# A loop of two steps for GpSimd's gathers in the edge loop of a graph attention layer

## What is computed

```python
h = (layernorm(x) @ W.T).reshape(n, 8, 32)
alpha = a_src . h[src] + a_dst . h[dst] + sum(relu(edge_attr @ edge_W.T + edge_b) * h[dst])
alpha = where(alpha >= 0, alpha, 0.2 * alpha)
ex = exp(alpha - segment_max(alpha, dst)[dst])
out = segment_sum(h[src] * ex / segment_sum(ex, dst)[dst], dst)
x = x + out + bias          # then the mixture of experts on layernorm(x)
```

## Time and profile before

| | us |
|---|---|
| median of 3 runs | 3645.68 |
| lowest and highest run | 3639.31, 3689.38 |
| the profiled execution | 3650.59 |
| its span, first to last instruction | 3648.7 |

### The profile page before, as it was taken

One profiled execution on the slowest core, in us unless ns is written; L12 is line 12 of the kernel. 1 busy time (PEld: TensorE's weight loads), 2 busy tenths in 40 slices (PEclk: granted clock), 3 DMA queues, 4 the chain that ended last, 5 costly groups with the idle time before them and its releaser, 6 DMA issues. The chain is left out here.

```text
span 3648.7 us, 35893 instructions
## 1 busy us (share of the span) xinstructions
PE 2371.3 (65%) x8642; PEld 1602.4 (44%) x8642; DVE 2272.9 (62%) x3546; ACT 985.6 (27%) x2822; POOL 1902.5 (52%) x2041
## 2 busy tenths in 40 slices
PE   1646766766666665766676766756666464269998
PEld 1424443433444443443444434434344243068887
DVE  7956776766667676776667767766666564352223
ACT  3522222222222222222222222222222221053332
POOL 3655655665665555565556655665555453507000
PEclk9857777777777777778767777787777777559999
DMA  8345555555555555555555545555555985200000
GB/s 272 111 136 140 155 144 142 148 144 156 155 151 142 151 143 146 140 149 163 147 137 154 150 133 143 154 149 164 147 141 148 119 121 83 79 14 24 17 20 30
DMA packets 341605, 471.09 MB, mean 129 GB/s; under 512 B 115596, under 2 KB 262718, under 8 KB 341170
## 3 DMA queue, kind: packets, MB, share of 16 engines
q0 software_dynamic: 90000, 262.14, 29.1%
q1 hardware_dynamic: 250578, 206.73, 19.8%
q10 hardware_dynamic: 848, 0.26, 0.0%
HBM read 380.17 MB, written 88.72 MB: 129 GB/s over the span
## 5 line engine op out<-in xcount | busy, mean ns | idle before, releaser
L999 POOL DMA_INDIRECT src_in<-t_node_rows,rec_in x1760 | 1678.7, 954 | 1230.2 <-DVE weighted L1256 635.9
L1061 PE MATMUL p_sum<-weighted,hot 128*128 128x264 f32 x3520 | 1207.8, 502 | 567.9 <-issue 366.6
L1061 PEld LDWEIGHTS p_sum<-weighted,hot 128*128 128x128 f32 x3520 | 841.1, 249 | 924.6 <-issue 595.2
L1206 DVE SCALAR_TENSOR_TENSOR prod<-p_enc,near 128x512 f32<-128x512 f32 x880 | 563.1, 681 | 577.8 <-ACT near L1128 316.1
L1256 DVE TENSOR_TENSOR weighted<-src_in,p_turn 128x1024 f32<-128x1024 f32 x440 | 534.6, 1215 | 295.8 <-remote 111.7
L1039 PE MATMUL p_pick<-win,hotT 128*128 128x272 f32 x880 | 389.5, 531 | 369.5 <-ACT near L1128 170.2
L1210 DVE TENSOR_REDUCE dots<-prod 128x32 f32<-128x1024 f32 x440 | 536.9, 1220 | 15.2
L1108 ACT ACTIVATE hot<-apart 128x128 f32<-128x128 f32 x440 | 136.2, 310 | 1299.9 <-PE p_sum L1061 604.3
L1128 ACT COPY near<-p_pick 128x272 f32<-128x272 f32 x440 | 169.4, 385 | 821.8 <-remote 494.6
L1039 PEld LDWEIGHTS p_pick<-win,hotT 128*128 128x128 f32 x880 | 156.6, 223 | 478.2 <-issue 297.8
L1032 PE MATMUL p_enc<-expander,attrT 30*128 30x256 bf16 x1760 | 310.6, 302 | 39.7 <-DMA attrT<-t_block_attr 37.8
(11 more groups left out here) (334 smaller groups left out, 1627.9 us busy)
## 6 DMA issues: line engine op xcount, KB each, us to landing
win<-t_node_rows SPq DMA_DIRECT2D x440, 136.0 KB
t_block_sums<-sums SPq DMA_DIRECT2D x110, 528.0 KB
places<-t_block_places SPq DMA_DIRECT2D x110, 256.0 KB
src_in<-t_node_rows,rec_in POOLq DMA_INDIRECT x1760
attrT<-t_block_attr SPq DMA_DIRECT2D x330, 36.0 KB
t_node_rows<-out_rows SPq DMA_DIRECT2D x49, 136.0 KB, 1.8
x<-in_x SPq DMA_DIRECT2D x4, 1536.0 KB, 25.6
out_x<-x SPq DMA_DIRECT2D x48, 128.0 KB
```

What stands on the lines that cost most here:

```text
L999: pool.indirect_dma_start(src[:, q.par, b, k, :], None, scr["rows"], bass.IndirectOffsetOnAxis(ap=rec_i[:, q.par, b, k:k + 1], axis=0)).th ...
L1061: last = nc.tensor.matmul(p_sum[b % 2][:, 0:ROW], hot[:, q.par, b, :], weighted[:, b, k, :], start=(k == 0), stop=(k == W - 1))
L1206: nc.vector.scalar_tensor_tensor(prod[:, 2 * half:2 * half + 2, :], p_enc[(PAIRS * b + half) % len(p_enc)][:, :, :], 0.0, near[:, q.par, b ...
```

## The change

POOL's steps of the edge loop are no longer written out one by one. A new function `loop` writes out the steps 0 and 1, then one `Fori` on POOL with (110 - 2 - 2) / 2 = 53 turns, whose body holds two steps, and then, as before, the last two steps and the early gathers of the merge (`last`). The steps in the body have expressions in the loop's register as `s` and `turn`; `par` stays a number, so the addresses of tiles and the semaphores of the gathers stay fixed. The values of the five waits of a step become expressions in the register. All other engines still use `steps`.

```diff
@@ -867,6 +867,16 @@
                 body(straight(k))
             last()
 
+        def loop(engine, body, last):
+
+            for k in range(RING):
+                body(straight(k))
+            turns = (STEPS - RING - 2) // RING
+            with engine.Fori(0, turns) as i:
+                for u in range(RING):
+                    body(Step(i * RING + RING + u).of(i + 1, u))
+            last()
+
         assert STEPS % RING == 0 and Q == 4
 
         turn = P // Q
@@ -1013,7 +1023,7 @@
-            steps(gather, last)
+            loop(nc.gpsimd, gather, last)
 
         @block.tensor
```

## The result

| us | before | after |
|---|---|---|
| median of 4 runs each | 3662.84 | 3719.83 |
| lowest and highest | 3639.31, 3689.38 | 3699.99, 3853.15 |
| the profiled execution | 3650.59 | 3705.42 |
| its span | 3648.7 | 3703.7 |

The account below looks back on a forecast made before the run. The prediction took the semaphore round between PE, ACT and DVE to bound each step, gathers beside it. From 3650.6 us, -5 for pauses, 0 for registers, 0 for turns gave 3645.6, as a median 3641 us; range 3612 to 3695.

Parts of the forecast that it names:

- Step 1, the pauses: POOL's gathers in the edge loop: program-fetch pauses, 28 us in all, vanish; a fifth, 5 us, gained.
- rival C: POOL's pauses count in full: 28 us back, 3618 us (0.12), or 3573 with half of SP's waits (0.04).
- Step 2, registers: POOL's register operations before the edge loop's waits: at most 64 us, hidden by the sequencer's lead, costed at 0.
- Step 3, the turn: POOL's jump back at the 53 loop turns: up to 74 us if refetched, but short body, costed at 0.
- rival A: Each of POOL's 53 turns costs a pause of 1.4 or 2.8 us: 3720 or 3794 us; chance 0.09.
- rival B: Smoother POOL lengthens slow times of SP and ACT by 15%, 74 us on ACT's waits: 3715 us; chance 0.04.
- the term for the slow times: POOL's register operations while sequencers are slow: 1.4 us per group, 148 us bound without lead, costed at nothing.

Follow-up runs that it names:

- e2: The changed kernel with POOL's loop turning only twice, 52 steps written out per turn, registers kept in the waits, against the kernel before: 3691.92 us, ratio 1.0093.
- e3: The written-out kernel before, with block 0's gathers also waiting for block 1's weighting, against the kernel before: 3888.17 us, ratio 1.0616.
- e8: The written-out kernel before, with block 0's gathers also waiting for DVE's next prod pair, about 1.3 us later, against the kernel before: 3749.81 us, ratio 0.9945.

## Why the prediction was wrong, point by point

**What bounds the kernel.** "What bounds a step is this round of semaphores between PE, ACT and DVE; the gathers run beside it" holds as a reading of the chip of the profile: after the change the gathers' landing is again only 56.6 us of DVE's idle time. What the sentence left out is how the gathers act on the round. They do not delay it as a predecessor; where they run on this chip, the news in it comes late (10% of SP's records slow at the start of a run of gathers, 51% from the ninth on). The chips C and D show the difference: without the slow times the same round is short enough that the gathers bound the loop.

**Step 1, the pauses (5 us gained).** Wrong in its cause. The pauses of 1.70 us are still there with a body of two steps that runs 53 times. POOL's timeline of the kernel after:

```profile
1375.97 0.94 POOL L1009 DMA_INDIRECT src_in<-t_node_rows,rec_in  x1 [0.43 <-issue]
1378.61 0.94 POOL L1009 DMA_INDIRECT src_in<-t_node_rows,rec_in  x1 [1.70 <-issue]
...
2397.22 0.94 POOL L1009 DMA_INDIRECT src_in<-t_node_rows,rec_in  x1 [0.82 <-DVE weighted L1266]
2399.86 0.95 POOL L1009 DMA_INDIRECT src_in<-t_node_rows,rec_in  x1 [1.70 <-issue]
```

Counting gathers, 13 such pauses stand in the kernel after and 14 in that before, and ten of them stand behind the very same gathers (the 113th, 201st, 553rd, 641st and so on, 88 or a multiple of it apart). They follow the count of gathers and not the place in the program. The prediction had the count of 88 and explained it by the program because the program's length goes with the gathers; the same rows fit both. The instruction queue's packets, which would have been the direct row, were 119 before and are 103 after: 16 fewer, not the end of a stream. On chip C there are only 4 and 5 of them (before and loop), all but one on the same grid. The 28 us were not on offer, nor was rival C, which is made of them.

**Step 2, registers (0 us).** Right as far as a delay goes, and better shown than predicted. Where DVE releases a group of gathers, the first one starts 0.812 us (median of 166 cases before, and of 160 after) behind the end of DVE's weighting, the same to 1 ns in both kernels: a wait on a register's value adds nothing there that can be told. On chips C and D, with no slack on POOL, the whole loop costs under 3 us. The price of POOL's register operations during the slow times, 0.7 us, did not appear either: the longest of 318 is 0.035 us. That registers have no part in the shift of the pattern is not shown; e2, which kept them and nearly all of the loss, points at them.

**Step 3, the turn (0 us).** Right. 0.050 + 0.032 + 0.045 us; e2 with two turns, and the chips C and D. By the trace the body of two steps is cheap to jump back to. The Trainium skill ("Runtime: NRT & Kernel Launch", "Instruction fetch mechanics") says that a taken branch has to fetch its target page first if that lies outside the two pages at hand; the 0.045 us agree with it as far as this short body goes. e2's body of 52 steps is far longer, but it turns back only once, so no run here shows what a jump back over more program costs.

**The rivals.** A (the turn pauses), which I gave most of the slower side, did not happen: the time near its 3720 us is a coincidence of sums. B (more of the slow times, 3715 us, 0.04) is nearest to what came. Its place was right in part, DVE's wait for `near`. Its mechanism, longer slow times by a smoother POOL, was not: the share of SP's slow records did not rise (17% against 19%), nor did the stretches of over 2.5 us in which semaphore updates or SP's operations follow each other at 0.64 to 0.735 us (some 80 of about 6 us in either kernel, from 600 to 2600 us, 450 to 500 us in all; the exact count hangs on how the stretches are joined, and on the missing records). They came about as often and hit the place behind `raw` in 57 steps instead of 34. That B's 3715 us lies near the measured time is luck.

**The range.** "Half of rival A above" is not what the range has: half of the 79 us between 3641 and 3720 ends at 3681, and the range goes to 3695. The measured 3719.83 lies outside by either.

**The step that failed** is the term for the slow times. The sum has it at nothing: it takes the steps' 26.3 us as fixed and asks only what is added to POOL or taken from it, and "Nothing shows that a loop would do it" left a longer round to rival B at 0.04. What the runs showed in its place is 23 more stalled steps of 97 at 2.8 us, 64 us of the 71 us by which these steps grew. That POOL's own waiting hides an operation holds for a delay. It does not cover a change in which moment the gathers start and stop relative to the round, and the prediction had the row for it: in the step of the earlier trace rows DVE stood still for 8.26 us while POOL went on gathering. I used that row to name the slow times and priced them by a guess of 15%, instead of asking how many of the 110 steps had such a stall (34 of 97) and what a step with and without it takes (27.5 and 24.7 us). The difference, 2.8 us times 97 steps, is the width that belonged into the range: if all steps stalled, 63 x 2.8 = 176 us more; if none did, 34 x 2.8 = 95 us less. The lower end is an estimate that no run reached: in e3 and e8, with 3 and 0 stalled steps, the time went elsewhere.

**What stays open.** Why the loop pushes the steps on chips like A from 35% to 59% stalled (34 to 57 of 97). What the rows give is that block 3's sums ran at the full clock in 58 steps instead of 34. Nothing in POOL's starts differs by a measurable delay, and nops do not do it. Registers in written-out waits were never run on a chip of that kind beside the loop, since the three comparisons made for it came to chips without stalls. Nor is it known what makes the news late on chips A and B and not on C and D; since those are also the traces that lack most update records, and every run here carries a granted clock and was thus recorded in some way, a part of the recording itself in the slow times is a rival that no run excludes. It is open too whether the gain of e8 on chip B would undo the loop's loss on A. No version measured here beats the kernel before by more than 0.6% anywhere.

## What to carry to other kernels

Before a wait or an operation is priced, sort the repeats of a loop by their length and see whether there are two kinds: a change that costs nothing can still shift how often the longer kind comes, and its price is then about the difference of the two times the share that moves. Before a releaser is believed, count the records that it is read from. A pause that comes every so many instructions may belong to the count of work (descriptors, transfers) as well as to the program; find a row that parts the two before it is put into a sum. And a loss of one per cent that is found on one chip should be looked for on a second, where the same instructions may wait for something else.

## What the runs showed of the hardware

- The same kernel takes 3066 us on two chips, 3664 on a third and 3768 on a fourth, with equal durations of POOL's and DVE's instructions (a gather 954 and 956 ns). On the third and the fourth 16 to 20% of SP's sequencer records last about 0.7 us (in e3 3%), the more of them the longer POOL gathers without a pause (10% at the first four gathers, 51% from the ninth on); on the first two at most 0.2% do. The cause was not tried.
- The traces of the third and fourth chip hold 22,787 to 26,865 records of semaphore updates, those of the first two 59,061 to 59,130, for nearly the same program.
- Indirect DMAs of 128 rows follow each other every 1.25 us on POOL, with a pause of 1.70 instead of 0.30 us at some places that lie 88 or a multiple of 88 gathers apart, loop or not: 13 and 14 in the two kernels, and 4 and 5 on chip C.
- POOL's register operations in a loop's waits cost 32 to 52 ns each and the branch back 45 ns, and the sequencer runs so far ahead of indirect DMAs that none of it is seen, even where POOL is the bound (0.9998, 0.9990 to 1.0007).
- PE at the lower clock goes with a shorter next step in the kernel before on a chip of A's kind: its eight sums take 3.80 instead of 2.02 us, the next gathers start later, and the stall of 9 us followed in 3 of 56 such steps, against 29 of 34 at the full clock.
